# Attention head by head: sums divided out per pair of heads, values turned in their projection, mask and counts scattered in pairs

## The reference

```python
h = jnp.maximum(_layernorm(x), 0.0)
q = h @ wq.T + bq;  k = h @ wk.T + bk;  v = h @ wv.T + bv
q2 = (q @ wiq.T + biq)   # and k2, v2: 16 heads of 64 columns each
mask = full(-inf); mask[src, dst] = softplus(edge_type_weights)[edge_type - 1]
...                      # diagonal cells that no edge fills get weight 3
scores = einsum('hnd,hmd->hnm', q2, k2) / 8 + mask
out = einsum('hnm,hmd->hnd', softmax(scores), v2)
x = x + out @ wo.T + bo
```

## Time and profile before

| what | value |
|---|---|
| median of 3 runs | 1020.43 us (1014.75 to 1021.98) |
| the profiled execution's own time | 1018.43 us |
| its span, first to last instruction | 1016.6 us |
| TensorE busy | 941.5 us, 93% |
| VectorE, GpSimd, ScalarE busy | 605.3, 484.6 and 367.3 us |
| mean granted clock of TensorE | 0.966 |
| DMA | 131.18 MB, mean 129 GB/s |

### The profile page before, as it was taken

How to read it: one execution, slowest core, us unless ns; L and a number is a source line. 1 busy time by engine, 2 the same in 40 slices (tenths; PEclk the granted TensorE clock), 3 DMA queues, 4 the chain that set the end, 5 groups by cost and what they waited for, 6 DMA issues and landing times.

```text
span 1016.6 us, 13971 instructions
## 1 busy us (share of the span) xinstructions
PE 941.5 (93%) x4743; PEld 841.1 (83%) x4743; DVE 605.3 (60%) x1043; ACT 367.3 (36%) x575; POOL 484.6 (48%) x409
## 2 busy tenths in 40 slices
PE   2999999994898979999999999999999969999994
PEld 2999999994797977888888888888888848887883
DVE  6888888862897344556455464554556464545625
ACT  5333333331686244322222222222225333334321
POOL 4133334775798443265374664755658203114312
PEclk9999999996999998999999999999999979999997
DMA  8966656531443526444544444444333513323301
GB/s 216 280 208 204 204 157 171 140 63 23 94 93 88 145 63 212 145 104 147 149 119 142 105 156 154 107 141 121 94 111 109 186 63 108 121 103 104 124 21 63
DMA packets 85784, 131.18 MB, mean 129 GB/s; under 512 B 22312, under 2 KB 63464, under 8 KB 85736
## 3 DMA queue, kind: packets, MB, share of 16 engines
q1 hardware_dynamic: 68800, 126.22, 39.6%
q0 software_dynamic: 15360, 0.08, 3.6%
q10 hardware_dynamic: 1576, 4.27, 1.3%
HBM read 116.65 MB, written 7.59 MB: 122 GB/s over the span
## 4 chain that ended last, share of the span: by engine, by line
PE 69%; DMA 18%; DVE 5%; issue 3%; POOL 3%; ACT 2%; ACTq 0%; DVEq 0%; POOLq 0%; SPq 0%
PE ps L571 48%; DMA mask_d<-type_val,cell 12%; PE ps L618 8%; PE ps L443 4%; DMA count_d<-met,cell 4%; PE ps L491 2%; PE ps L515 2%; PE ps L422 1%; PE ps L502 1%; POOL count_d L1446 1%; DVE stats L1015 1%; DMA b_in<-in_L_gnn_bo 1%; PE ps L480 1%; PE ps L722 1%; PE ps L433 1%
## 5 line engine op out<-in xcount | busy, mean ns | idle before, releaser
L1136 DVE TENSOR_TENSOR wlo<-raw,whi 128x1024 fp32r<-128x1024 f32 x120 | 198.2, 1655 | 143.2 <-ACT whi L828 143.1
L443 PE MATMUL ps<-acts,whi 128*128 128x384 f32 (+1 forms) x896 | 229.9, 337 | 4.4 <-DVE acts L1116 4.4
L1485 POOL TENSOR_TENSOR mean_lo<-mean_f,mean_hi 128x384 fp32r<-128x384 f32 x80 | 89.4, 1118 | 189.7 <-ACT mean_hi L927 189.7
L443 PEld LDWEIGHTS ps<-acts,whi 128*128 128x128 f32 x896 | 162.4, 189 | 4.6 <-issue 4.6
L443 PE MATMUL ps<-acts,wlo 128*128 128x384 f32 (+1 forms) x448 | 150.3, 336 | 0.0
L927 ACT ACTIVATE mean_hi<-mean_f 128x384 fp32r<-128x384 f32 x80 | 42.0, 526 | 298.1 <-DVE mean_f L1249 298.1
L571 PE MATMUL ps<-whi,mean_hi 128*128 128x512 f32 x480 | 149.0, 392 | 0.0
L571 PE MATMUL ps<-whi,mean_lo 128*128 128x512 f32 x480 | 147.8, 389 | 0.0
L571 PE MATMUL ps<-wlo,mean_hi 128*128 128x512 f32 x480 | 147.8, 389 | 0.0
L828 ACT ACTIVATE whi<-raw 128x1024 fp32r<-128x1024 f32 x120 | 125.4, 1049 | 22.3 <-PE ps L571 21.7
L571 PEld LDWEIGHTS ps<-wlo,mean_hi 128*128 128x128 f32 x480 | 90.2, 188 | 19.9
(11 more groups left out here) (154 smaller groups left out, 1543.8 us busy)
## 6 DMA issues: line engine op xcount, KB each, us to landing
raw<-in_L_gnn_weight SPq DMA_DIRECT2D x64, 512.0 KB, 3.3
rows_b<-rows_d SPq DMA_DIRECT2D x24, 384.0 KB, 5.1
raw<-in_L_gnn_w_gate SPq DMA_DIRECT2D x16, 512.0 KB, 3.3
raw<-in_L_gnn_W_self SPq DMA_DIRECT2D x16, 512.0 KB, 3.3
raw<-in_L_gnn_W_neigh SPq DMA_DIRECT2D x16, 512.0 KB, 3.3
count_d<-total_r SPq DMA_DIRECT2D x8, 576.0 KB, 4.2
rel_r<-count_d SPq DMA_DIRECT2D x8, 576.0 KB, 4.4
raw<-in_L_gnn_wq SPq DMA_DIRECT2D x32, 128.0 KB, 7.0
```

The lines of the kernel that those rows point to most:

```text
L443: mm = pe.matmul(ps[:, j % 2, 0:N], stationary[j % RING][:, k, :], acts[:, a, moving, k, :], start=i == 0, stop=i == 3 * KT - 1)
L1136: dve.tensor_tensor(wlo_row[slot], raw[slot][:, :], whi_row[slot].bitcast(F32), ALU.subtract)\
L1485: pool.tensor_tensor(mean[1][:, k % 2, :], mean_f[:, k % 2, :], mean[0][:, k % 2, :].bitcast(F32), ALU.subtract).then_inc(S["mean_lo"], 1)
```

## The change

- The mask's chunks, the counts' and the edge weights' are scattered in pairs (`GROUP = 2`): the first of a pair waits until all before it have landed, the second does not wait for the first. So that both never write one cell, `meet` and `sum_weights` compare with 256 edges, and edges that are not to count go to spare cells of their own. All chunks of the mask come first, then all of the counts.
- `stage_scores` copies four blocks per head: q high and k high onto the head's own 64 rows, q low and k high onto the other 64. One matmul over 128 rows then gives high x high + low x high; a second one, on 64 rows straight from `acts`, gives high x low. A row tile takes two matmuls instead of three.
- The last projection's output is evacuated in one piece (`v_f`), turned by three transposes per tile while the next tile is multiplied, and split after it. `stage_v` copies one head at a time, in runs of 64 values where they were 128, onto a `v_st` whose other 64 columns are zero; both heads of a pair then add up in one PSUM bank.
- The exponentials are not scaled. `invert_sums` writes each row's inverted sum 64 times over into `rinv`, `spread_sums` turns it with three transposes per pair, ScalarE copies it out (`read_spread`), and VectorE multiplies the pair's output with it (`make_pair`). The pair is split at full height (`pair_high`, `pair_low`).
- The loops over heads are written out, and the scores of the head after next come ahead of a head's transposes on TensorE.
- At the start x comes first on SP's queue, all edges first on ScalarE's, and the biases go through GpSimd's queue; their transpose moves behind the activations'. The softplus moves behind the first copies. GpSimd makes the first weight tile's residual. The mask's base is stored two tiles later, and the zeroing of the count planes goes from tile 12 on, every second tile. `q_st` and `k_st` lie in `rel_r`, and `sparse_w` in `mask`.

```diff
-    LAG = 30
+    GROUP = 2
...
+        def landed(eng, signals, c):
+
+            for q in range(GROUP):
+                need(eng, signals[q], 16 * ((c - q + GROUP - 1) // GROUP))
+
+        def others(c):
+
+            g = c // GROUP % (CHUNKS // GROUP)
+            return slice(GROUP * P * g, GROUP * P * (g + 1)), slice(P * (GROUP - 1 - c % GROUP),
+                                                                    P * (2 * GROUP - 1 - c % GROUP))
...
-                    sp_.wait_ge(S["mask_base_made"], 1 + NT)
-                    sp_.dma_start(plane(mask_d, 0), mask[:, :, :]).then_inc(S["mask_based"], 16)
                 if t == 4:
                     key_rows(2)
                     key_rows(3)
+                    sp_.wait_ge(S["mask_base_made"], 1 + NT)
...
+            def stage_scores(o):
 
                 r0 = DH * (o % 2)
-
-                need(sp_, S["scores_ready"], (i * 4 + (o - 1)) * NT)
-                sp_.dma_start(q_st[r0:r0 + DH, :, o % 2, :].bitcast(F32),
-                              acts[r0:r0 + DH, 0, :, i * 2 + o // 2, :].bitcast(F32))\
-                   .then_inc(q_staged[o % 2], 16)
+                need(sp_, S["scores_ready"], (o - 1) * NT)
+                for staged, a, part, to in ((q_st, 0, 0, r0), (k_st, 1, 0, r0),
+                                            (q_st, 0, 1, DH - r0), (k_st, 1, 0, DH - r0)):
+                    sp_.dma_start(staged[to:to + DH, o % 2, :].bitcast(F32),
+                                  acts[r0:r0 + DH, a, part, o // 2, :].bitcast(F32)).then_inc(q_staged[o % 2], 16)
+
+            def stage_v(o):
+
+                d0 = DH * (o % 2)
+                sp_.wait_ge(S["v_hi"], o // 2 + 1)
+                sp_.wait_ge(S["v_lo"], o // 2 + 1)
+                need(sp_, S["pv_done"], o - 1)
+                sp_.dma_start(v_st[:, o % 2, :, :, d0:d0 + DH].bitcast(F32),
+                              v_rows[:, :, :, DH * o:DH * o + DH].bitcast(F32)).then_inc(v_staged[o % 2], 16)
...
+            landed(sp_, mask_scattered, EC)
...
+            stage_v(0)
+            stage_v(1)
+            for o in range(2, H):
+                stage_scores(o)
+                if o >= 4:
+                    stage_v(o - 2)
+            stage_v(H - 2)
+            stage_v(H - 1)
...
+            pe.wait_ge(S["bcol_in"], 16 * 7)
+            pe.wait_ge(S["start_lo"], 1)
+            pe.transpose(ps[:, 2, 0:7 * KT], b_in[:, :], ident[0:7 * KT, 0:7 * KT]).then_inc(S["bcol_made"], 1)
...
+            def turn_v(j):
+
+                pe.wait_ge(S["v_made"], j + 1)
+                need(pe, S["v_lo"], j - 1)
+                for m in range(NT):
+                    mm = pe.transpose(ps[:, 6 + j % 2, P * m:P * m + P], v_f[:, j % 2, P * m:P * m + P], ident[:, :])
+                mm.then_inc(S["v_turned"], 1)
+
+            def value_tiles(g):
+                for j in range(KT):
+                    if KT - 3 <= j < KT - 1:
+                        turn_weight(g + 1, j + 3 - KT)
+                    if j < 2:
+                        pe.wait_ge(S["out_lo"], g * KT + (j - 1 + O_CREDIT))
+                    else:
+                        pe.wait_ge(S["v_made"], j - 1)
+                    column_tile(g, j, 3)
+                    if j:
+                        turn_v(j - 1)
...
+            def scores(o):
+                r = DH * (o % 2)
+                pe.wait_ge(q_staged[o % 2], 64 * (o // 2 + 1))
                 for nt in range(NT):
 
-                    need(pe, S["scores_read"], (i * 4 + (o - 1)) * NT + (nt + 1))
-                    for n, (a, c) in enumerate(((0, 0), (0, 1), (1, 0))):
-                        mm = pe.matmul(ps[:, nt, 0:N], q_st[:, a, o % 2, P * nt:P * nt + P],
-                                       acts[:, 1, c, i * 2 + o // 2, :], start=n == 0, stop=n == 2)
+                    need(pe, S["scores_read"], (o - 1) * NT + (nt + 1))
+                    if o == 0:
+                        if nt < 2:
+                            pe.wait_ge(S["v_made"], KT - 1 + nt)
+                        else:
+                            pe.wait_ge(S["w_lo"], T_WO + 2)
+                    rows_of = slice(P * nt, P * nt + P)
+                    pe.matmul(ps[:, nt, 0:N], q_st[:, o % 2, rows_of], k_st[:, o % 2, :], start=True, stop=False)
+                    mm = pe.matmul(ps[:, nt, 0:N], acts[r:r + DH, 0, 0, o // 2, rows_of],
+                                   acts[r:r + DH, 1, 1, o // 2, :], start=False, stop=True)
                     mm.then_inc(S["scores_ready"], 1)
...
+            def spread_sums(pair):
+
+                pe.wait_ge(S["sum_inverted"], 2 * pair + 2)
+                if pair:
+                    pe.wait_ge(S["spread_read"], pair)
+                else:
+                    pe.wait_ge(S["v_lo"], KT)
+                for nt in range(NT):
+                    mm = pe.transpose(ps[:, 7, P * nt:P * nt + P], rinv[:, pair % 2, nt, :], ident[:, :])
+                mm.then_inc(S["spread_made"], 1)
+
+            def weigh_values(o):
+                pair, e = divmod(o, 2)
+                if e:
+                    spread_sums(pair)
+                elif pair:
+                    pe.wait_ge(S["pair_made"], pair)
+                else:
+                    pe.wait_ge(S["v_lo"], KT - 1)
+                    pe.wait_ge(S["v_cleared"], 2)
+                pe.wait_ge(S["pt_lo"], (o + 1) * NT)
+                pe.wait_ge(v_staged[e], 16 * (pair + 1))
                 n = 0
                 for m in range(NT):
                     for a, c in ((0, 0), (0, 1), (1, 0)):
-                        mm = pe.matmul(ps[:, 6 + o % 2, 0:N], v_st[:, o // 2 % 2, a, m, :],
-                                       pt[c][:, o % 2, m, :], start=n == 0, stop=n == 3 * NT - 1)
+                        mm = pe.matmul(ps[:, 6, 0:N], v_st[:, e, a, m, :], pt[c][:, o % 2, m, :],
+                                       start=e == 0 and n == 0, stop=e == 1 and n == 3 * NT - 1, skip_group_check=True)
                         n += 1
                 mm.then_inc(S["pv_done"], 1)
 
-            def head(i, o):
-                turn_probs(i, o)
-                if exists(i, o + 2):
-                    scores(i, o + 2)
-                if not is_head(i, o, 0):
-                    weigh_values(i, o - 1)
-
-
-            pe.wait_ge(S["out_lo"], O_CREDIT + 6 * KT)
-            pe.wait_ge(S["w_lo"], T_WO + 2)
-            scores(0, 0)
-            for m in range(NT):
-                turn_v(m)
-            scores(0, 1)
-            pe.wait_ge(S["v_hi"], NT)
-            pe.wait_ge(S["v_lo"], NT)
-            head(0, 0)
-            with pe.Fori(0, 3) as i:
-                for o in range(1, 5):
-                    head(i, o)
-            for o in range(1, 4):
-                head(3, o)
-            weigh_values(3, 3)
-
-
-            pe.wait_ge(S["head_lo"], O_CREDIT + H)
+            scores(0)
+            turn_v(KT - 1)
+            scores(1)
+            for o in range(H):
+                if o + 2 < H:
+                    scores(o + 2)
+                turn_probs(o)
+                if o:
+                    weigh_values(o - 1)
+            weigh_values(H - 1)
...
+            act.wait_ge(S["ones_made"], 1)
+            act.activation(std[:, 0, :], epsc[:, :], ACT.Sqrt).then_inc(S["ones_made"], 1)
...
+            def v_high(j):
+                act.wait_ge(S["v_turned"], j + 1)
+                act.activation(v_rows[:, 0, :, P * j:P * j + P],
+                               ps[:, 6 + j % 2, 0:N].rearrange("p (t d) -> p t d", t=NT), ACT.Copy)\
+                   .then_inc(S["v_hi"], 1)
...
+            def read_spread(pair):
+                need(act, S["pair_lo"], pair - 1)
+                act.wait_ge(S["spread_made"], pair + 1)
+                act.activation(o_f[:, pair % 2, :], ps[:, 7, 0:N], ACT.Copy).then_inc(S["spread_read"], 1)
+
+            def pair_high(pair):
+                act.wait_ge(S["pair_made"], pair + 1)
+                act.activation(acts[:, 0, 0, pair, :], o_f[:, pair % 2, :], ACT.Copy).then_inc(S["pair_hi"], 1)
...
+            def invert_sums(o):
+                dve.wait_ge(S["exp_ready"], (o + 1) * NT)
+                d0 = DH * (o % 2)
+                dve.reciprocal(rinv[:, o // 2 % 2, :, d0:d0 + DH],
+                               rsum[:, o % 2, :].unsqueeze(2).to_broadcast([P, NT, DH])).then_inc(S["sum_inverted"], 1)
...
+            def make_pair(pair):
+                dve.wait_ge(S["spread_read"], pair + 1)
+                dve.wait_ge(S["pv_done"], 2 * pair + 2)
+                dve.tensor_tensor(o_f[:, pair % 2, :], ps[:, 6, 0:N], o_f[:, pair % 2, :], ALU.mult)\
+                   .then_inc(S["pair_made"], 1)
+
+            def pair_low(pair):
+                dve.wait_ge(S["pair_hi"], pair + 1)
+                dve.tensor_tensor(acts[:, 0, 1, pair, :], o_f[:, pair % 2, :], acts[:, 0, 0, pair, :].bitcast(F32),
+                                  ALU.subtract).then_inc(S["pair_lo"], 1)
...
+            for o in range(H):
```

(48 more changed lines are left out.)

435 lines of the change are left out of this document (195 added, 240 removed).

## The result

| | before | after |
|---|---|---|
| median of 14 runs each | 1017.68 us | 1010.29 us |
| lowest to highest | 1012.67 to 1021.98 | 1004.86 to 1012.65 |
| profiled execution: its own time, span | 1018.43, 1016.6 us | 1011.11, 1009.4 us |
| first projection tile starts | 23.50 us | 22.23 us |
| last projection matmul ends (T) | 226.96 us | 228.15 us |

The ratio is 0.9928, 95% interval 0.9908 to 0.9948. The change makes the kernel faster by 0.7% (7.4 us), which the interval tells from none, and by less than the 1% that the forecast set as its bound. 1010.29 us lies outside of the range (977 to 1005). The forecast took 30.5 us off a median of 3 runs, 1020.43; over 14 runs the kernel before takes 1017.68, so 7.4 us stand against 30.5. By the table's row on the attention, that stretch became shorter by 9.9 us instead of 29.5.

A forecast was written before the change was run, and what follows sets the result against it. TensorE, busy 93% of 1016.6 us, was taken as the bound, apart from a 14.6 us mask wait. Attention -29.5, moved transposes +2.0 and start -3.0 gave -30.5: span 986.1, with run overheads 990 us; range 977 to 1005.

The forecast's parts named there:

- The mask: Scatter before the attention: pairs at 5.4 us, ending near 178 us, mask in near 216 us, 14.6 us wait gone.
- The values' transposes: Projections: 24 transposes of value tiles, six groups ahead of the last projection tile, adding 2.0 us there.
- A head on TensorE: Attention: six score matmuls (1.06 us) for nine (1.62 us), a head's sum 3.77 us against 4.17.
- A head on VectorE: Attention: 4.60 us a head with pair work and a wide reciprocal of about 1.35 us, setting the pace.
- Staging: SP's queue in the attention: a 5.3 us path from weighing to staged blocks, where 5.4 us are there.
- Rival (b): Attention: staging sets the pace through landings of 4.4 to 6 us; 1001 us, or 1008 at 8 us; chance 0.20.
- Value pieces of 256 B: Staging of values: pieces of 256 B for 512 B, taken to cost nothing; bounds nothing or 1.5 us more.
- The sum: Attention, last projection tile's end to `wo`'s first transpose: 77.1 us instead of 106.6, a gain of 29.5 us.
- the opening to the first head's transposes: Start of the attention: head 2 staged at T + 6.1, its scores and head 0's transposes ending at T + 8.2.
- the tail: End of the attention: a reciprocal, the last two heads' residuals and two weighings, 7.2 us.
- The start: Before the first projection tile: biases off the critical queue, first tile at 20 to 21 us, -3.0 us, bounds 0 and -5.
- Rival (d): Attention: short pauses in every head halve TensorE's clock, 7.5 us a head, +44 us, 1034 us; chance 0.04.

The follow-up runs named there:

- single ones: The changed kernel with one scatter to a step in place of pairs, all the mask's still ahead of the counts': 1046.23 us, ratio 1.0288.
- one shape: The changed kernel with the second score product over all 128 rows instead of 64, so not computing the reference's scores: 994.84 us, ratio 0.9819.
- in place: The changed kernel with no q or k staged, nine score matmuls of 64 rows a head straight from `acts`: 993.82 us, ratio 0.9747.
- the opening filled: The changed kernel with nine idle matmuls between the scores of head 1 and those of head 2: 1006.49 us, ratio 0.9924.
- merged staging: Two score transfers of 192 KB per head for four of 96 KB: on the changed kernel 1005.91 us (0.9920), with all score products over 128 rows 991.47 us (0.9750).

## Why the prediction was wrong, step by step

**The mask: right.** The wait is gone. A pair took 6.5 us (24 pairs from 41.75 to 190.86 us start to start of the last, 23 steps, `cells` included) where I had 5.4 and 0.4 for `cells`, and the first went out at 41.75 us instead of 38, so the last scatter goes out at 192.1 us instead of 178; the load of the mask at 211.60 us was queued behind `wo`'s tiles as said. A pair is only a fifth cheaper than two single scatters (4.0 us each in the run with single ones).

**The values' transposes: right.** The projections' stretch, first tile to T, grew from 203.5 to 205.9 us; +2.4 for +2.0.

**A head on TensorE: the step that failed.** It reads "nine score matmuls (1.62 us) become six (1.06 us, one of the two of each output on 64 rows but with the same 384 columns)". I priced a matmul by its columns and its row in a chain where all had 128 rows; there was no mixed one in the trace, I did not bound it, and so it entered neither the sum nor the rivals. Measured: 2.22 us, through changes of row count at 0.2 us each, six of them a head. The run with one shape takes them away, and the ratio falls by 1.1%. The Trainium skill (TensorEngine Tiling (Array Packing), Key Properties) states that a change of the tiling mode, unlike a change of tile within it, drains the engine. It gives no time for it; the distances 0.37 and 0.175 agree with it, and so do the weight loads, which wait for the matmul before them only where the row count changes. I had not weighed that rule. Besides, the sum 3.77 left out the transitions between groups: 27 or 30 matmuls in 4.62 us in place, where the same terms add up to 4.33. The kernel before had shown such a rest already, 4.17 by the sum and 4.36 by the row.

**A head on VectorE: right, and not what decides.** The reciprocal took 1.34 us, forecast 1.35. With the scores in place VectorE was busy 39.41 of 40 us at 4.62 us a head, forecast 4.60.

**Staging: half right.** The issues took 0.60 us, and where TensorE waited the path was 5.0 to 6.5 us from the end of a weighing, forecast 5.3. That "it fits by a tenth" was too kind: once the matmuls were of one shape, TensorE waited 10.5 us in eight places. Rival (b) was the second limit, hidden behind the first; with one shape, merging the transfers took another 0.7% off the ratio.

**Value pieces of 256 B: right, as far as the trace can say.** The landing took 2.6, 2.7 and 6.8 us (least, median, most of 16) against 2.9, 3.1 and 4.9 before. But a landing carries 192 KB now, where it carried 384 KB in as many pieces: half the bytes for 0.87 of the time, so what a smaller piece costs by itself is not shown. The 1 us more that I weighed by the rule of 512 B is not in the median. The Trainium skill (DMA: Bandwidth & Descriptors, "Why small descriptors are slow (HBM only)") limits that rule to transfers with HBM; these go from SBUF to SBUF, and the row does not speak against it.

**The sum, at `wo`'s first transpose:** 324.86 us for 303.1, 21.8 late. The first tile +1.7, the projections +0.5, the opening to the first head's transposes +2.6 (T + 9.8 for T + 7.2), thirteen periods +16.5 (75.4 us for 58.9), the tail +0.5. Four of the thirteen, at half clock in whole or in part, took 28.1 us; the nine from 251.34 to 298.59 us 5.25 each. Two runs at full clock split the 16.5. With the opening filled thirteen take 68.0 us, so 7.4 are the half clock's; with one shape and merged staging they take 58.5, so another 9.5 are the changes of shape and the staging. In the medians the order is plain: one shape is worth 1.1%, merged staging with it 0.7%, and filling the gap nothing that can be told.

**The start: near the forecast, and scattered.** I had the first tile at 20.5 us. It came at 22.23 us in the profiled execution and at 20.57 to 21.35 in the ten others with this start, six of them below 21; the kernel before has one trace, 23.50. What the traces differ in is the arrival of the edges, which land behind x now and held VectorE 2.2 to 4.1 us. I had followed the biases, which landed in 2.0 to 3.8 us and held nothing, and not what else was moved behind x. The comparisons took 0.13 us more each as said (479 against 345 ns), and they (TensorE 50.00 of 50 us from 150 to 200) and all behind `wo` (+1.4 us) were covered.

**Rival (d)**, the clock, had 0.04 on the argument that every fall follows a gap of 3 us or more. That held for the trace before and not here: it falls after 1.62 us, and again after 1.75 us at 301.4. The rival came true in part: the attention's mean granted clock is 0.89. But the gaps of 0.4 to 0.6 us among the heads left it at 1.00, so the swinging at frequent short pauses, which I had weighed from the Trainium skill (TensorE: Matmul & The Clock Gate, "A second HAM failure mode: psum-queue depth-cycling"), is not in the trace.

## What to carry to other kernels

Price a matmul by its neighbours too: where the number of rows changes from one to the next, add what a change costs (0.2 us here), and keep matmuls of one shape together or make them all one shape, even if that takes more of them. Before copying operands to save matmuls, add up the copies' path as a rival limit: nine matmuls in place beat the six alternating ones with staging (0.9747 against 0.9928) and are level with six of one shape (0.9750). When something is moved ahead in a queue, follow what it now stands in front of to its last reader, as the counts and the edges showed; and a pace that two engines set almost alike shows no gain when one is relieved.

## What the runs showed of the hardware

- Changes between 64 and 128 rows cost 0.2 us of TensorE time each at full clock (matmuls of 384 columns), because the weight load no longer runs beside the matmul before it; within one row count 64 rows go at the same 0.175 us as 128.
- A gap of 1.62 us, after which TensorE was busy 94% of 15 us, was followed by 13.7 us at half clock. Gaps of 1.85 and 2.11 us in the merged kernel of one shape were not: the length of a gap alone does not tell. In place, a gap of 1.34 us was followed by 3.4 us at half clock.
- Two indirect scatters in flight take 6.5 us, one 4.0: a second one hides 1.5 us of 8.
- A reciprocal of 192 elements per partition takes 1.34 us, the copy that repeats three elements 64 times 0.29 to 0.37.
